# One order written out for five engines, exchanged for another: a two-layer attention kernel on one core

## The reference

```python
# layer 0
cmod = silu(c) @ w_ada + b_ada          # six vectors for each batch
x_mod = layernorm(x) * (1 + scale_msa) + shift_msa
k, q, v = split(x_mod @ w_qkv, 3)       # 16 heads of 8
w = softmax(q / 8 @ k.T);  y = w @ v
x = x + gate_msa * (y @ w_proj + b_proj)
h = gelu((layernorm(x) * (1 + scale_mlp) + shift_mlp) @ w_mlp1 + b_mlp1)
x = x + gate_mlp * (h @ w_mlp2 + b_mlp2)
# layer 1
row_zero = x.sum(-1) == 0
self_feat = concat(x, where(row_zero, 0, c)) @ W_self.T + b_self
output = self_feat
for d in range(2):
    A = (adj if d == 0 else adj.transpose(0, 2, 1, 3))[:, :, :20, :]
    aff = (q1 @ k1.T) / sqrt(8)         # 16 heads, 20 keys
    aff = where(A.sum(-1) > 0, aff, -9e15) + (A @ w_bias + b_bias)
    output = output + softmax(aff) @ kv, through Wout[d], + bout[d]
x = x + relu(output)
```

## Time and profile before

| | |
|---|---|
| median of three runs | 96.94 us (96.56 to 97.03) |
| the profiled execution | 95.63 us, its span 93.8 us |
| TensorE busy | 83.7 us of the span |
| VectorE busy | 71.7 us |
| ScalarE busy | 55.7 us |
| GpSimd busy | 46.1 us |
| granted clock of TensorE | 0.987 on average |

### The profile page before, as it was taken

The page is one execution under the profiler, slowest core; times in us unless marked ns, Lnnn a source line. Parts: engine busy times, 40 slices in busy tenths (PEclk is TensorE's granted clock), DMA queues, the critical chain, the costliest instruction groups (busy, mean ns, idle before and its releaser), DMA issues.

```text
span 93.8 us, 4196 instructions
## 1 busy us (share of the span) xinstructions
PE 83.7 (89%) x1802; PEld 67.5 (72%) x1802; DVE 71.7 (76%) x183; ACT 55.7 (59%) x127; POOL 46.1 (49%) x72
## 2 busy tenths in 40 slices
PE   4959989999999989989999999999998999968900
PEld 4849967676676778768888877988876688647800
DVE  0766289989699997689169388997989879568791
ACT  4880386939999729572972305789244597208620
POOL 6697015457922005546242461081553977971680
PEclk9999999999999999999999999999999999999995
DMA  1989999400000000000000001100200212120203
GB/s 35 246 203 367 372 232 241 112 3 7 0 7 7 0 7 3 0 0 0 7 0 0 5 20 31 30 10 22 55 9 0 57 31 64 27 54 14 61 0 112
DMA packets 3778, 5.75 MB, mean 61 GB/s; under 512 B 720, under 2 KB 2896, under 8 KB 3632
## 3 DMA queue, kind: packets, MB, share of 16 engines
q1 hardware_dynamic: 3496, 5.31, 20.6%
q10 hardware_dynamic: 264, 0.18, 0.7%
HBM read 4.22 MB, written 0.52 MB: 51 GB/s over the span
## 4 chain that ended last, share of the span: by engine, by line
PE 65%; DVE 15%; issue 6%; POOL 5%; ACTq 4%; ACT 2%; POOLq 0%; DVEq 0%
PE ps_s L1043 8%; PE ps_b L964 8%; PE ps_b L944 7%; PE ps_b L919 6%; PE ps_b L895 5%; PE ps_b L1069 5%; ACTq L752 4%; PE ps_b L1061 4%; PE ps_b L970 4%; PE ps_b L1091 3%; PE ps_b L912 3%; POOL E L676 3%; DVE neg_max L1445 3%; PE ps_b L1100 2%; PE ps_b L952 2%
## 5 line engine op out<-in xcount | busy, mean ns | idle before, releaser
L1227 ACT ACTIVATE PT<-ps_b 120x384 f32<-120x384 f32 x16 | 7.4, 487 | 8.6 <-PE ps_b L1061 4.6
L1141 ACT ACTIVATE hidden<-ps_b,cols 128x256 f32<-128x256 f32 x16 | 7.0, 474 | 6.5 <-PE ps_b L964 6.5
L856 POOL TENSOR_TENSOR rstd<-var_eps,minus_half 128x2 f32<-128x2 f32 (+1 forms) x9 | 6.0, 668 | 6.3 <-DVE var_eps L1261 6.2
L784 POOL TENSOR_TENSOR Kb<-k_raw,head_mask 128x640 f32<-128x640 f32 x4 | 5.0, 1258 | 8.1 <-ACT k_raw L1156 5.4
L1436 DVE TENSOR_TENSOR E<-ps_s,bias_rep 128x640 f32<-128x640 f32 x8 | 6.6, 823 | 3.0 <-PE ps_b L1061 1.7
L964 PE MATMUL ps_b<-xm,w_rest_sb 128*128 128x256 f32 x32 | 8.6, 385 | 0.0
L676 POOL TENSOR_TENSOR E<-E,neg_max 128x640 f32<-128x640 f32 x5 | 6.4, 1271 | 4.4 <-DVE neg_max L1445 3.9
L1043 PE MATMUL ps_s<-Kb,home_b 32*32 32x80 f32 x512 | 7.4, 239 | 0.7 <-DVE E L1436 0.7
L970 PE MATMUL ps_b<-hidden,w_rest_sb 128*128 128x256 f32 x32 | 7.6, 386 | 0.0
L647 POOL TENSOR_TENSOR xm<-xm,cmod 128x256 f32<-128x256 f32 (+1 forms) x6 | 3.5, 586 | 8.3 <-DVE xm L1283 8.3
L1043 PEld LDWEIGHTS ps_s<-Kb,home_b 32*32 32x32 f32 x512 | 5.7, 103 | 2.4 <-issue 1.5
(11 more groups left out here) (120 smaller groups left out, 218.0 us busy)
## 6 DMA issues: line engine op xcount, KB each, us to landing
w_rest_sb<-in_w_rest SPq DMA_DIRECT2D x1, 1088.0 KB, 7.9
home_a<-in_adj SPq DMA_DIRECT2D x2, 448.0 KB, 12.3
Vz<-v_raw SPq DMA_DIRECT2D x16, 33.8 KB
xT<-in_xT SPq DMA_DIRECT2D x1, 512.0 KB, 9.8
home_a<-in_adj SPq DMA_DIRECT2D x1, 512.0 KB, 12.7
out<-x_tok SPq DMA_DIRECT2D x3, 128.0 KB, 1.9
x_tok<-in_x_tok SPq DMA_DIRECT2D x1, 256.0 KB, 5.2
w_ada_sb<-in_w_ada SPq DMA_DIRECT2D x1, 256.0 KB, 5.6
```

The lines of the kernel that those rows point to most:

```text
L856: ins = pool.tensor_tensor(rstd[:, layer, g0:g1], var_eps[:, layer, g0:g1], minus_half[:, 0:g1 - g0], ALU.pow)
L1141: return act.activation(hidden[:, slot_of(h), j, 0:n], ps[:, 0:n], ACT.Gelu_apprx_tanh, bias=cols[:, R_MLP1 + j:R_MLP1 + j + 1])
L1227: ins = act.activation(PT[0:KR, key % 3, 0:CH, :], ps[0:KR, 0:CH * P].rearrange("p (j t) -> p j t", t=P), ACT.Exp)
```

## The change

Only tables are changed: `FILL`, `ON`, `TAKE_ON`, `BANKS` and `ORDER`. The steps themselves, their shapes and their data stay. The lines of the code move down by 2, so line 1043 of the kernel before is 1045 in the changed one.

```diff
-FILL = {('k', 0): 12, ('xnT', 2): 2}
+FILL = {('xnT', 0): 2, ('q', 0): 5, ('xnT', 2): 4, ('k', 2): 2}
 ON = {...
- ('shift', (0, 0)): 'dve',
+ ('shift', (0, 0)): 'pool',
- ('spread', ('k1', 1, 0)): 'act',
- ('spread', ('k1', 1, 1)): 'pool',
+ ('spread', ('k1', 1, 0)): 'dve',
+ ('spread', ('k1', 1, 1)): 'act',
- ('spread', ('v1', 3, 1)): 'act',
+ ('spread', ('v1', 3, 1)): 'sp',
- ('sub', 12): 'dve',
+ ('sub', 12): 'pool',
+ ('zero', 'vz1a'): 'act',
...
-ORDER = [('zero', 'v1_ones'), ('consts', 0), ('zero', 'v0_ones'), ('zero', 'pad'), ('ident', 0), ('masks', 0), ('plus1', 0),
+ORDER = [('zero', 'v0_ones'), ('ident', 0), ('zero', 'v1_ones'), ('masks', 0), ('consts', 0), ('zero', 'pad'), ('silu', 0),
```

More of the change, by code:

```diff
@@ L180 @@
+ ('xnT', 3): 3,
  ('q', 2): 2,
[L181 to L187, removed]
- ('q', 4): 1,
- ('values', 0): 0,
- ('v', 4): 2,
+ ('turn', 0): 3,
+ ('v', 3): 0,
+ ('k', 3): 1,
+ ('q', 3): 2,
+ ('v', 2): 0,
+ ('values', 0): 2,
+ ('q', 4): 1,
+ ('turn', 1): 0,
+ ('k', 4): 3,
+ ('v', 4): 1,
+ ('yT', 0): 2,
+ ('turn', 3): 1,
  ('turn', 2): 3,
[L192 to L195, removed]
+ ('proj', 0): 2,
  ('values', 1): 3,
- ('bias', 0): 2,
+ ('turn', 5): 2,
@@ L198 @@
  ('x1tok', 0): 1,
  ('turn', 4): 3,
- ('turn', 5): 0,
- ('values', 2): 0,
- ('values', 3): 3,
+ ('bias', 0): 0,
+ ('values', 2): 3,
+ ('values', 3): 2,
  ('xn2T', 0): 1,
- ('turn', 6): 3,
+ ('turn', 7): 3,
+ ('yT', 1): 2,
+ ('turn', 6): 1,
  ('yT', 2): 0,
- ('turn', 7): 1,
- ('yT', 1): 2,
  ('mlp1', 0, 0): 3,
+ ('proj', 1): 2,
  ('proj', 2): 0,
[L210 to L213, removed]
+ ('mlp1', 0, 2): 1,
+ ('mlp1', 0, 3): 2,
+ ('mlp1', 0, 1): 0,
  ('x1tok', 2): 3,
- ('values', 4): 2,
@@ L216 @@
- ('x1tok', 1): 0,
- ('mlp2', 0): 1,
- ('yT', 3): 2,
+ ('values', 4): 1,
+ ('x1tok', 1): 2,
+ ('mlp2', 0): 0,
+ ('yT', 3): 1,
  ('xn2T', 2): 3,
[L220 to L229, removed]
- ('q1', 0, 1): 3,
[L231 to L237, removed]
+ ('xn2T', 1): 2,
@@ L238 @@
+ ('proj', 3): 1,
+ ('rowsum', 0): 0,
+ ('self', 0): 3,
+ ('mlp1', 2, 2): 2,
+ ('mlp1', 2, 0): 0,
+ ('mlp1', 1, 2): 1,
+ ('q1', 0, 0): 2,
+ ('k1', 0, 0): 0,
+ ('k1', 0, 1): 3,
+ ('mlp1', 1, 1): 1,
+ ('v1', 0, 0): 2,
+ ('mlp1', 2, 1): 3,
+ ('mlp1', 1, 3): 1,
+ ('x1tok', 3): 0,
+ ('mlp1', 1, 0): 2,
+ ('q1', 0, 1): 3,
  ('mlp1', 2, 3): 1,
- ('v1', 0, 0): 3,
  ('mlp2', 1): 2,
[L241 to L245, removed]
- ('x2tok', 2): 1,
- ('rowsum', 2): 3,
@@ L248 @@
[L248 to L273, removed]
@@ new lines @@
+ ('xn2T', 3): 0,
+ ('mlp2', 2): 1,
+ ('self', 1): 0,
+ ('rowsum', 1): 2,
+ ('mlp1', 3, 1): 1,
+ ('mlp1', 3, 3): 3,
+ ('rowsum', 2): 2,
+ ('q1', 1, 0): 0,
+ ('self', 2): 3,
+ ('k1', 1, 1): 2,
+ ('k1', 1, 0): 1,
+ ('v1', 1, 0): 0,
+ ('k1', 2, 1): 2,
+ ('q1', 1, 1): 1,
+ ('mlp1', 3, 0): 2,
+ ('q1', 2, 0): 0,
+ ('q1', 2, 1): 1,
+ ('v1', 2, 0): 2,
+ ('mlp1', 3, 2): 0,
+ ('turn', 9): 0,
+ ('mlp2', 3): 2,
+ ('turn', 8): 1,
+ ('k1', 2, 0): 3,
+ ('turn', 10): 3,
+ ('rowsum', 3): 1,
+ ('turn', 11): 2,
+ ('x2tok', 3): 0,
@@ new lines @@
+ ('self', 3): 3,
+ ('values', 6): 1,
+ ('values', 5): 0,
+ ('q1', 3, 1): 3,
+ ('k1', 3, 0): 2,
+ ('turn', 13): 2,
+ ('v1', 3, 0): 3,
+ ('k1', 3, 1): 0,
+ ('turn', 12): 2,
+ ('turn', 14): 3,
+ ('turn', 15): 1,
+ ('sbtok', 0): 0,
+ ('x2tok', 0): 2,
+ ('values', 7): 3,
+ ('values', 8): 0,
+ ('sbtok', 1): 1,
+ ('q1', 3, 0): 2,
+ ('turn', 17): 1,
+ ('turn', 16): 2,
+ ('sbtok', 2): 3,
+ ('x2tok', 2): 1,
+ ('x2tok', 1): 2,
+ ('turn', 18): 3,
+ ('turn', 19): 0,
+ ('sbtok', 3): 1,
+ ('values', 9): 1,
+ ('values', 10): 3,
```

278 lines of the change are left out of this document (130 added, 148 removed), and 7 rows, old and new, of the table ORDER.

## The result

The changed kernel takes 97.17 us (median of 12 runs, 96.43 to 98.71) beside 96.44 for the kernel before (median of 12, 95.41 to 97.8). The ratio is 1.0103 (95% interval 1.0064 to 1.0142); a second comparison of 12 and 23 runs gives 1.0095 (1.004 to 1.015). The forecast was 94.8. The runs of either kernel lie within some 3 us, and a ratio compares the faster, undisturbed ones only, so the medians of all runs are given beside it where they say something else. Here they do: they are 0.8% apart in the first comparison and equal in the second (97.25 and 97.25). So the changed kernel gains nothing by either measure, and how much it loses, up to 1%, depends on the measure. The profiled execution takes 96.59 us and spans 94.8; before it was 95.63 and 93.8.

What follows compares the result with a forecast made beforehand. TensorE's nearly unbroken work was taken as the floor, leaving only holes to gain. Start -0.7, more work ahead +2.6, VectorE work -2.0 and idle -2.0 gave -2.1: median 94.8 us from 96.94, range 92.9 to 97.3.

Steps and rivals of the forecast that it cites:

- start: Program start through q, k and v of chunk 0: between 1.5 us gained and 0.2 lost, taken as 0.7 gained.
- more work ahead of the first `badd`: Ahead of layer 1's first scores: 2.6 us more TensorE work, so the first `badd` comes at 58.0 instead of 56.07.
- VectorE's work in the stretch: First `badd` to last `mult`: 6.7 us of steps out, 4.5 in; net written as 2.0 us less.
- idle time there: First `badd` to last `mult`: about 2 of VectorE's 5.5 us idle go, with `v1` transfers off ScalarE.
- last `mult`: End of VectorE's layer-1 softmax stretch: at 88.5 us instead of 90.6, the sum of terms being -2.1.
- the hole at 80 us: ScalarE issues four `v1` transfers for 4.01 us; exponentials behind them start late and TensorE waits 1.15 us.
- rival (a): More gain than counted: VectorE's stretch with 2 us idle rather than 3.5, plus a fast start; 92.9 us, chance 0.15.
- The transfers on SyncE's queue: Eight in a row, 6 us, last landing before 84.5 for values wanted at about 84: cost 0 to 1.2, taken as 0.
- Weight loads at the slow pace behind 10 us: Sign of a wrong forecast, at the start: TensorE's weight loads still at four in half a microsecond.
- Rival (b): Start gives nothing and 2 us idle return as waits for GpSimd's `sub`: 96.9 us, no change; chance 0.12.
- Rival (c): Slower: VectorE's stretch starts late, idles 5.5 us, meets GpSimd for 1.7; median 99, or 98.4 with half; chance 0.13.
- meetings: VectorE steps waiting beside GpSimd steps, at a residual and a `yb`: about 0.7 and 1.0 us of waiting.

Runs made afterwards that it cites:

- Run 13: Changed kernel with each layer-1 unit's scores replaced by two products of ones, 896 TensorE instructions fewer: 0.9775 of the kernel before; medians 95.43 beside 96.90 us.
- run 7: Changed kernel with the tile of ones written ahead of the identity on GpSimd: 0.995 of the kernel before.
- 14: Kernel before with each layer-1 unit's scores replaced by two products of ones: ratio 1.0003; medians 96.03 beside 96.90 us.
- Run 6: Kernel before with its 14 products of ones each cut in three, 112 TensorE instructions more: ratio 1.1639.
- run 11: Kernel before with addition `yb` of group 0 and the second residual of mid 3 on GpSimd instead of VectorE: ratio 0.9892.
- run 4: Kernel before with only the four `v1` (3,1) transfers moved to SyncE's queue: medians 99.29 beside 97.25 us.
- run 5: Changed kernel with the same columns of ones in products of up to 512 columns, 44 TensorE instructions fewer: 0.9737 of the kernel before; medians 95.93 beside 97.07 us.

## Why the prediction was wrong

By its own sum, on the profiled executions:

| term | forecast | measured |
|---|---|---|
| start | -0.7 | +1.0 (first scores 14.46 after 13.47) |
| more work ahead of the first `badd` | +2.6 | +2.7 (3.7 in all, less 1.0 of the start), 0.36 of it the stall at 32.78 |
| VectorE's work in the stretch | -2.0 | -2.7 (29.00 to 26.27) |
| idle time there | -2.0 | +0.3 (5.53 to 5.79) |
| last `mult` | -2.1 | +1.2 (90.60 to 91.83) |

**The step that failed is the idle time**, 2.3 us of the 3.3 missed. One half of it was right: the hole at 80 us went, and putting it back costs 2.7 us in this order. But in "about 2 us of VectorE's 5.5 idle go" I took it that nothing comes in its place. VectorE idled 5.79 us, nearly all in waits for TensorE, and three stalls of TensorE for its own instructions, 0.60, 1.02 and 0.53 us, 2.15 in all, stand on the chain ahead of 2.68 us of these waits.

How much of the loss the stalls make is not settled. 2.15 us is the most. Run 13, with 1.46 us less of them, has a stretch shorter by 0.88; there, and in run 7, TensorE waits 0.74 and 1.64 us for the transfers of `v1` instead. So the next limit lies close behind the stalls, and no run here comes down to the 3.5 us of idle time in the sum: run 13 still has 4.97, with 0.67 us of stall left.

What ties the stalls to the change, by argument, is its other part: the long products that stood among the small ones behind the first scores now stand ahead of them, so the same small products follow closer. For the same count of instructions (2241 to 3521) the kernel before needed 20.9 us, from 67.18 to 88.11; the changed kernel went through it in 18.9, from 69.74 to 88.68, with 2.1 of them stalls. Runs 13 and 14 bear it out in their profiles. That "the work is missing behind them" was my reason for rival (a); by this argument it is also what brings the stalls.

**The start** is a term outside its bounds (-1.5 to +0.2). Its times were right up to 7.5 (the last five ones began at 7.52, forecast 7.25). The pace was not: the ten pieces took 2.50 us, where I had counted 2.1 although has ten such pieces at 2.50, and q, k and v took 1.07, so that the block ended at 11.10 and not between 9.0 and 10.7. Of the 0.8 us beyond my bound, 0.4 shows at the end of that block, and 0.4 comes behind it, where TensorE waits 0.38 us for the take of chunk 1 (to 11.59) ahead of four products of ones. One execution of each kernel overstates the term: over all profiles with the old start the first scores came at 13.27 to 14.30, 13.76 on average (six), with the new one and narrow products at 14.12 to 14.98, 14.52 on average (four), so that some 0.8 us are lost and not 1.0. The Trainium skill, TensorE: Matmul & The Clock Gate, section Part 1: The HAM clock gate, says that the clock follows how busy the array has recently been; the prediction took that rule as worth 0.9 us against the change. The rise did come later on average, in the same four profiles at 10.0 to 12.4 us after 9.1 to 11.3 in the six, but the ranges overlap, so that the part of the gaps in it is not shown. Run 6 is a row that the rule as I had it does not foresee: 15.6 us without a gap, and no rise.

**VectorE's work** was right in kind and larger than counted (2.7 for 2.0). That it shortens the end one for one was not shown by any row: run 11 takes 2.1 us of it away and gets 0.4 of the stretch. **The work ahead of the first `badd`** measured 2.7 for 2.6, and that is partly luck, since 0.36 of it is a stall that the sum did not have.

**The transfers on SyncE's queue** cost nothing in the two profiles of the changed kernel, as forecast. But the cover was thin: TensorE waited 1.64 us for them once the start was earlier (run 7), 0.74 with fewer stalls (run 13) and 3.5 in the old order (run 4). The term was nothing in an execution in which other terms had gone wrong, and that part of its success is luck.

Of the signs named: no step of two SBUF operands above 1 us on VectorE behind 60, no transfer on ScalarE's queue, were right. Weight loads at the slow pace behind 10 us, and a first `badd` behind 59, were the signs of a wrong forecast, and both came. A stall of 1.0 us between 80 and 86 came too, not from ScalarE. The measured 97.17 lies inside the stated range (92.9 to 97.3), at its slow end. Rival (b), 96.9, is nearest: the start gave nothing and the 2 us of idle time came back as waits, but for TensorE and not for GpSimd's `sub`, which no turn waited for by 0.2 us or more. (Its sum put 1.4 us for what its words call 2; with 2 it is 97.5.) Rival (c) had the sign, the late stretch and an idle time of 5.5 us; what it added for meetings, 1.7 us, did not come, and its point of decision, a stretch over 32.6 us, was not reached (32.06).

Two versions beat both kernels: the changed one with the tile of ones first and wide products of ones (0.982 and 0.989 of before), and the old order without the two meetings (0.989).

## What to carry to other kernels

Before a long step is moved out of a stretch of small products, count TensorE's instructions in what is left, four for each small float32 product: here no 256 of them went through in under 2.8 us, five in a row with stalls took about 4 us each (run 5), and an order that closes other waits can run into that. When one limit is taken away, look for the next: here the stalls hid a wait for transfers. A stall marked "issue" in the middle of a row of like products, at the same count in two profiles, is such a place; look for the instruction queue's packet, which ended 1.2 to 1.6 us before TensorE went on. And a sum of busy time and idle time of one engine is not a forecast: take each microsecond of idle time that is to go and name what the engine waits for next.
